# Placing a median search, two strided convolutions and their fillers anew on five engines of one core

## The reference, cut to what matters

```
q_in = quantile(x.reshape(16, 64, -1), 0.5)          # median of each channel's 128x128 pixels
x = x + relu(-q_in)                                  # then: up by 2, relu, down by 2, a 7-tap filter on each
xf = x + irfft2(rfft2(x) * gate)                     # gate: two small matmuls on the magnitudes
q = xf_flat @ q_w + q_b                              # 4 heads of 16
k1, v1 = kv_path(conv 8x8, stride 8)                 # 256 keys: conv, layernorm, kv matmul, 3x3 depthwise on v
k2, v2 = kv_path(conv 16x16, stride 16)              # 64 keys
out = softmax(q @ k.T / 4) @ v                       # 16384 queries, 320 keys
y = out @ proj_w + proj_b + x
```

## Time and profile before

| what | value |
|---|---|
| median of 3 runs | 11242.98 us (11229.0 to 11243.66) |
| the profiled execution, its own time | 11240.24 us |
| its span | 11238.7 us |
| PE busy | 10118.1 us, 90% of the span |
| DVE busy | 8624.4 us, 77% |
| ACT busy | 7246.8 us, 64% |
| POOL busy | 5892.8 us, 52% |
| mean granted PE clock | 0.96 |

### The profile page before, as it was taken

How to read it: one execution, slowest core, us unless ns; L and a number is a source line. 1 busy time by engine, 2 the same in 40 slices (tenths; PEclk the granted TensorE clock), 3 DMA queues, 4 the chain that set the end, 5 groups by cost and what they waited for, 6 DMA issues and landing times. The chain is left out here.

```text
span 11238.7 us, 198959 instructions
## 1 busy us (share of the span) xinstructions
PE 10118.1 (90%) x68889; PEld 4971.5 (44%) x69001; DVE 8624.4 (77%) x14560; ACT 7246.8 (64%) x12221; POOL 5892.8 (52%) x10577
## 2 busy tenths in 40 slices
PE   2898998989989899899989989899898998989989
PEld 1534435344353543535345353443534435354353
DVE  7777777877778777778777777777787777777777
ACT  5757566665666656667666676656666666675665
POOL 2374463735537365472744737446373553736547
PEclk9999999999999999999999999999999999999999
DMA  2031231312314032140322303123131331403214
GB/s 67 21 78 47 58 85 32 77 36 64 79 32 88 26 73 70 39 89 35 71 54 49 94 22 78 45 59 84 32 79 34 67 76 32 88 32 70 66 40 102
DMA packets 330611, 664.69 MB, mean 59 GB/s; under 512 B 95624, under 2 KB 241160, under 8 KB 308048
## 3 DMA queue, kind: packets, MB, share of 16 engines
q1 hardware_dynamic: 329552, 651.29, 24.4%
HBM read 232.53 MB, written 71.30 MB: 27 GB/s over the span
## 5 line engine op out<-in xcount | busy, mean ns | idle before, releaser
L1314 ACT ACTIVATE R<-ps 128x512 f32<-128x512 f32 x5120 | 2874.7, 593 | 1432.3 <-PE ps L807 1034.8
L1095 DVE TENSOR_REDUCE R<-ps 128x2 f32<-128x640 f32 x3840 | 3042.7, 819 | 798.0 <-PE ps L786 748.7
L265 ACT ACTIVATE R<-R,st 128x1475 bf16<-128x1475 f32 (+1 forms) x1326 | 2077.1, 1566 | 494.9 <-DVE st L337 470.2
L326 DVE TENSOR_SCALAR_CACHE_REDUCE R<-R,st 128x1255 bf16<-128x1255 f32 (+1 forms) x1326 | 1936.9, 1461 | 18.5
L786 PE MATMUL ps<-KST,R 96*128 96x320 bf16 x7680 | 1699.7, 302 | 33.2 <-DMA R<-R 18.3
L807 PE MATMUL ps<-R,KST 104*128 104x512 bf16 x4096 | 1602.5, 394 | 82.7 <-DMA R<-Wk 25.5
L832 PE MATMUL ps<-R 128*32 128x512 f32 x12288 | 1663.2, 615 | 0.0
L1411 POOL TENSOR_TENSOR R<-R 128x256 f32<-128x256 f32 x1440 | 1059.1, 735 | 115.2
L1415 POOL TENSOR_TENSOR R<-R 128x256 f32<-128x256 f32 x1440 | 1050.2, 729 | 120.0
L786 PEld LDWEIGHTS ps<-KST,R 96*128 96x128 bf16 x7680 | 737.4, 99 | 647.7 <-DVE R L1095 154.8
L807 PEld LDWEIGHTS ps<-R,KST 104*128 104x128 bf16 x4096 | 398.4, 98 | 1247.6 <-ACT R L1314 952.5
(11 more groups left out here) (225 smaller groups left out, 19927.3 us busy)
## 6 DMA issues: line engine op xcount, KB each, us to landing
R<-R SPq DMA_DIRECT2D x3072, 64.0 KB, 2.4
R<-xh_in SPq DMA_DIRECT2D x136, 512.0 KB, 4.5
out_dram<-Z SPq DMA_DIRECT2D x68, 1024.0 KB, 3.9
R<-Wk SPq DMA_DIRECT2D x960, 64.0 KB, 2.0
Wk<-Wk SPq DMA_DIRECT2D x960, 64.0 KB, 2.0
R<-xa_in SPq DMA_DIRECT2D x36, 1024.0 KB, 9.9
R<-xb_in SPq DMA_DIRECT2D x36, 1024.0 KB, 11.7
R<-sr_in SPq DMA_DIRECT2D x32, 1024.0 KB, 5.1
```

Source lines behind the costliest of these rows:

```text
L265: e.activation(junka[:, 0:o2 - o1], xc[:, o1:o2], ACT.Sign, bias=mid, scale=-1.0, accum_out=ca[i]).then_inc(md_ca, 1)
L326: e.tensor_scalar(junk[:, 0:o1 - o0], xc[:, o0:o1], mid, None, ALU.is_le, ALU.add, accum_out=cv[i]).then_inc(md_cv, 1)
L1095: e.tensor_reduce(MX[(4 * u + s4) % 2][:, blk_, h0:h0 + 2], ps[:, 2 + 2 * bq:4 + 2 * bq, 0:320], axis=AX.X, op=ALU.max).then_inc(mx, 1)
L1314: e.activation(PB[:, t % 2, w, :], ps[:, w % 2, :], ACT.Exp).then_inc(ex, 1)
```

## The change

Only the placement of work changes. No operation of the reference is dropped or added; some result-less `busy` matmuls are added. On PE a slot now follows every second tap of the first convolution, and then every six taps of the second. The stages stand after taps 3, 9 and 15. Four `first_maxima` instead of eight lie between taps of the second convolution. One 512-column filler follows each of the later ones, and four precede the scores. The second hunk of the diff is PE's list, the third DVE's, the fourth POOL's slots after its stages, the last ACT's. DVE, POOL and ACT get the matching order, and `FIRST` has the two entries (1, 0) and (1, 1) two places earlier.

```diff
-FIRST = [(0, i) for i in range(13)] + [(1, 0), (1, 1)] + [(0, i) for i in range(13, 16)] + [(1, 2), (1, 3)]
+FIRST = [(0, i) for i in range(11)] + [(1, 0), (1, 1)] + [(0, i) for i in range(11, 16)] + [(1, 2), (1, 3)]
...
-                if n in (1, 3, 5):
-                    stage(0, n // 2 + 1, (4, 5, 3)[n // 2])
-                slot(1 if n > 5 else 0)
+                slot(n % 2)
+                if n in (3, 9, 15):
+                    stage(0, n // 6 + 1, (4, 5, 3)[n // 6])
             op.then_inc(c1_ps, 1)
             first, second = keys(0), keys(1)
-            conv2(0, 4)
-            slot(2)
-            conv2(4, 8)
+            conv2(0, 6)
             next(first)
-            conv2(8, 20)
+            for n in range(6, 24, 6):
+                conv2(n, n + 6)
+                slot(1)
+            next(first)
+            for n in range(24, 42, 6):
+                conv2(n, n + 6)
+                slot(1)
+            next(first)
+            for n in range(42, 66, 6):
+                conv2(n, n + 6)
+                slot(1)
+            next(first, None)
+            for n in range(66, 84, 6):
+                conv2(n, n + 6)
+                slot(1)
+            conv2(84, 92)
             slot(1)
-            conv2(20, 28)
-            next(first)
-            conv2(28, 44)
+            conv2(92, 100)
             slot(1)
-            conv2(44, 56)
-            next(first)
-            conv2(56, 76)
-            slot(1)
-            conv2(76, 84)
-            next(first, None)
-            conv2(84, 88)
-            for k in range(8):
-                conv2(88 + 5 * k, 93 + 5 * k)
+            conv2(100, 104)
+            for k in range(4):
+                conv2(104 + 6 * k, 110 + 6 * k)
                 first_maxima(k)
             next(second)
+            first_maxima(4)
+            busy(6, 2)
+            next(second)
+            first_maxima(5)
+            busy(6, 1)
+            first_maxima(6)
+            busy(6, 1)
+            next(second)
+            first_maxima(7)
+            busy(6, 1)
             first_maxima(8)
             busy(6, 1)
-            next(second)
-            first_maxima(9)
-            first_maxima(10)
-            next(second)
-            first_maxima(11)
-            busy(6, 2)
             next(second, None)
-            for k in range(12, 16):
+            for k in range(9, 14):
                 first_maxima(k)
+                busy(0, 1)
...
             lay_max(0)
-            for k in range(16, 20):
+            for k in range(14, 20):
                 first_maxima(k)
+                busy(0, 1)
+            busy(0, 4)
...
             for j in range(4):
                 stage(0, j, (6, 4, 5, 3)[j])
-                slot((4, 4, 4, 13)[j])
+                slot((3, 3, 4, 6)[j])
             first, second = keys(0), keys(1)
             next(first)
-            slot(1)
+            slot(3)
             next(first)
-            slot(1)
+            slot(3)
             next(first, None)
-            slot(1)
-            for k in range(8):
+            slot(6)
+            for k in range(4):
                 first_maxima(k)
             next(second)
-            first_maxima(8)
-            first_maxima(9)
+            first_maxima(4)
+            first_maxima(5)
             next(second)
-            first_maxima(10)
+            first_maxima(6)
+            first_maxima(7)
             next(second, None)
-            for k in range(11, 20):
+            for k in range(8, 20):
                 first_maxima(k)
...
-                slot((4, 4, 4, 16)[j])
+                slot((3, 3, 4, 18)[j])
...
+            e.wait_ge(xf, 16)
             for j in range(4):
                 stage(0, j, (6, 4, 5, 3)[j])
-            e.wait_ge(xf, 16)
-            bias(0, 56)
+                if j < 3:
+                    bias(3 * j, 3 * j + 3)
+            bias(9, 25)
             e.wait_ge(xt_ps, 16)
             first, second = keys(0), keys(1)
             next(first)
-            bias(56, 64).then_inc(zb, 1)
+            bias(25, 37)
+            next(first)
+            bias(37, 52)
+            next(first)
+            bias(52, 62)
             next(first, None)
-            next(second)
-            next(second, None)
+            bias(62, 64).then_inc(zb, 1)
+            for _ in range(4):
+                next(second, None)
```

More of the change, by code:

```diff
@@ L1261, in keys @@
                 e.activation(XQ[:, s0:s1_], ps[0:64, p1, 0:m], ACT.Sqrt, bias=c("eps", 64)).then_inc(ka[s], 1)
+                yield
                 e.wait_ge(kp[s], 4)
```

## The result

The changed kernel takes 11107.01 us (median of 4 runs, 11104.05 to 11113.07) against 11242.06 us (4 runs, 11229.0 to 11243.66); the ratio is 0.9882, with a 95% interval of 0.987 to 0.9895. The forecast was 11139 us with a range of 11105 to 11190: the sign held and so did most of the mechanism (what did not is told further down), and the gain of 135 us lies near the far end of the range, where 103 us was expected. The profiled execution took 11104.33 us, its span is 11103.0 us, and its mean granted clock is 0.971 (0.96 before).

The account below looks back on a forecast made before the run. PE, busy 90% of the span, was taken as the bound through its waits and slow clock. Five marks gave 6.7 us, taken as 6.5 over 16 passes: 104 us off 11240.2, plus 2.7, is 11139 us; range 11105 to 11190.

Parts of the forecast that it names:

- Mark 1: End of the first convolution: PE no longer waits for masks; 20.8 us after the first projection, 7.8 us earlier.
- Mark 2: Start of `keys(1)`: 25.7 us after the first convolution's end, 7.4 us earlier than before.
- The new wait at line 696: In `keys(0)`: PE waits 1.2 us for the chain of table load, square root, reciprocal and scaling.
- The cover of the biases: ACT's bias additions, moved between its stages in the list, end before ACT's next wait, so they cost nothing.
- Mark 3: First `lay_max`: 11.6 us after `keys(1)` starts, DVE coming last; 5.6 us earlier than before.
- Mark 4: First scores: 5.2 us after the first `lay_max`, set by PE's maxima and fillers; 4.1 us earlier than before.
- Mark 5: Second `lay_max`: some 4.8 us after the first scores, at full clock; 6.7 us earlier than before.
- 1.00 from mark 1 on: Expected sign in the profile: PE's granted clock stays at 1.00 from the end of the first convolution.
- the rival of a brief fall: Clock falls about 7 us between `keys(1)` and first scores; saving about 3.5 us a pass, 11187 us; chance 0.15.
- The rival of fillers in the way at half clock: Clock stays down from near `keys(1)` past the scores, fillers delay them; slower, 11265 us; chance 0.04.
- a late search: POOL's pace still sets the masks, delaying `load_unit(1)` and the transfer of `lay_max(0)`; at worst 11243 us; chance 0.03.
- The rival "more than I count": Mask sums free beside 64-column taps, DVE has slack in `keys(1)`; 8 us a pass, 11115 us; chance 0.16.

Follow-up runs that it names:

- the repeated run: The changed kernel run once more, unaltered, on the chip of three of the other runs: 11104.1 us, ratio 0.9883 against the kernel before.

## Why the prediction was right, and where its sizes were off

**Mark 1.** Right on the wait: with the slots of the change PE no longer waits for masks, wherever the stages stand, and the spreading of the stages alone gives less than a third of the 8.2 us. The prediction named the spacing; the earlier start of the mask sums, which it did not price, is part of it too. The size was 0.4 us short from misread prices that nearly cancel. The prediction read from the earlier trace rows that two taps take 1.04 us with and without a mask sum. The 1.04 us without one runs to the start of a stage; between taps, two take 0.91 (1.83 / 2, from 1240.70 to 1242.53), and the mask sum costs 0.13 here too. Four taps with a mask sum are 1.96 us instead of 2.08, and the four stages cost some 0.1 us more each than the 1.05 assumed.

**Mark 2.** The distance was forecast at 25.7 us and is 26.0. The new wait at line 696 came where it was put and for the reason given, but took 1.85 us instead of 1.2: PE reached it sooner. The mask sums between the 64-column taps cost 0.13 us (1250.99 to 1251.12) and not 0.2, and twelve taps passed in 1.36 us (1249.63 to 1250.99), 0.113 each instead of 0.125. The cover of the biases, priced as holding, does hold as placed; in one block it fails at 8 us a pass. The table load starts when the last bias ends (1246.09 + 3.60 = 1249.69), takes 1.28 us, and the root follows 0.02 us after it (1249.69 + 1.28 = 1250.97, root at 1250.99). The Trainium skill ("ScalarE: Activation LUTs", What ACT_TABLE_LOAD costs) adds a drain of about 1.38 us to the load. The trace does not agree: neither ahead of the load nor behind it is there time for one, and the sum was right to go by the row.

**Mark 3.** 11.6 us forecast, 11.5 measured, but this is luck. The forecast let DVE set it, with 1.9 us more work ahead than before. Where the clock stays up, DVE does set it, and the same list takes 10.50 us (three passes of the run with line 692 earlier, and all passes of the two other runs with the early root), 0.8 more than the 9.7 of before that the forecast started from. In the changed kernel the clock falls in every pass about 53 us after the first projection. The last first maxima of tile 0 and the fillers between them then pass at half clock, one pair every 0.85 us, DVE waits for them (0.54 and 0.16 us in the rows above), and `lay_max` comes after 11.0 to 11.7 us. DVE's part was priced 1.1 us too high, and 1.0 us that the forecast had at nothing came from the clock.

**Mark 4** is the term that was mis-sized most. The prediction gave PE 5.2 us between `lay_max` and the scores; it took 4.0. The prices of the first maxima at 2.4 GHz were taken from rows that overlap their neighbours or ran at half clock: 0.33 for the 256-key kind and 0.65 for the 64-key kind. They cost 0.23 (1283.19 to 1283.42) and 0.25 (1284.96 to 1285.21). The reason was wrong as well in one point: that the fillers cost 1.4 us beyond the transfer. Without any fillers the scores start 3.76 us after `lay_max`, so the fillers delay them by 0.3 us; and leaving four of them out moves the scores and not the second `lay_max`, as DVE is the later one.

**Mark 5.** 5.3 us from the scores instead of 4.8, for the same reason: the loop's maxima queue behind the last first maxima on DVE. Both errors partly cancel.

**The sum.** 7.9 us to mark 5 instead of 6.7: +0.4 from mark 1, -0.3 from mark 2, +0.1 from mark 3, +1.2 from mark 4, -0.5 from mark 5, and 0.3 because the second pass of before (74.80 us) was shorter than its mean (75.12). Taking 6.5 as the mean over passes went the wrong way. Another 0.8 us a pass is gained behind mark 5 (686.3 - 677.6 - 7.9), where I had said both do the same. The way from mark 5 to the next pass's first projection is 611.2 us before and 610.4 after, but it is 610.6 in the repeated run and 610.4 to 611.9 in the other variants, whose code there is the same. What sets it was not tested and stays open. 16 passes would make 139 us of it; the two traces' spans are 136 us apart, as the prologue ahead of the first pass is 2.8 us longer after.

**The clock.** "1.00 from mark 1 on" was wrong: it falls twice, to 0.72 in 6 us and 0.66 in 5 us. The first fall costs next to nothing: inside it 12 taps take 1.37 us (1255.73 to 1257.10, granted clock 0.50) where they took 1.36 at full clock. The second costs about 1.0 us a pass at mark 3, some 16 us a run (an estimate: the mean of 11.5 us less the 10.50 where the clock stays up). The prediction had named a clock at 1.2 GHz under the fillers as a sign of being wrong; for those ahead of mark 3 it came true. The clock is up again at the scores, and that is the part that pays: 29 us (36 by the ratios) when it is taken away, 36 us when it alone is added to the kernel before. So the rival of a brief fall was right that it falls and that this lies on the path, at 1.0 us where it had 2 to 3. The rival of fillers in the way at half clock came about for a few of them and not for the ones ahead of the scores; a late search did not come. The rival "more than I count" is nearest to what came, 8.7 us a pass. Its causes were not quite the ones it named: the mask sums are cheap but not free, DVE's slack in `keys(1)` was spent on the falling clock, and the most came from shorter matmuls at 2.4 GHz.

## What to carry to other kernels

When side work is woven into a dense engine's list, ask which engine sets the side work's pace, and give it room for more than that pace. Here the new slots of the mask sums (one per four taps instead of two, and from tap 1) are worth 96 us with the large pieces close together (11205.4 against 11109.7) and 59 us with them spread (11166.1 against 11107.0), and how these were spread no longer mattered once that was so. Each wait removed moves the next deadline forward: a block of cheap work of 16.5 us on an engine that works in order was free before and would have cost the whole gain after. When a mark lands where it was forecast, look all the same which engine set it: passes of one trace that differ only in the clock show it. Price a step that will run at another clock from the distance between starts at that clock, not from a length in a row, and look which engine is last at each mark before counting a delay.

## What the runs showed of the hardware

The 64-column fp32 taps hardly feel PE's clock: 24 instructions of line 677 passed in 1.36 us at a granted clock of 1.00 (1249.63 to 1250.99) and in 1.37 us at 0.50 (1255.73 to 1257.10), while the row of one of the scores' bf16 matmuls went from 0.39 to 0.61 us. And a row's length is not a matmul's price: a mask sum of four 128-column bf16 matmuls, 0.30 us long by its own row, moves the next start by 0.13 us, both between the 256-column taps (1240.57 to 1240.70) and between the 64-column ones (1250.99 to 1251.12). The taps read their input with a stride, every eighth or sixteenth element of a row; whether that sets their pace was not tried.
